# A decoder layer's cross attention: steps of two key chunks for one query block, one PSUM bank for the values, three for the other matmuls

## The reference

```
x = x + self_attention(layernorm(x))          # rotary, causal, one head of 128
x = x + cross_attention(layernorm(x), ctx)    # 16 heads of 64, keys and values from ctx, then Wo and a bias
x = x + ffn(layernorm(x))                     # rounded to 127 levels, ternary weights, bias
```

## Time and profile before

| | us |
|---|---|
| median of 3 runs | 1188.72 (1188.53 to 1189.51) |
| the profiled execution | 1185.61 |
| its span, first to last instruction | 1183.6 |
| busy: PE, DVE, ACT, POOL | 1141.1, 931.6, 692.8, 231.7 |
| granted TensorE clock, mean | 0.986 |

### The profile page before, as it was taken

One profiled execution on the slowest core, in us unless ns is written; L12 is line 12 of the kernel. 1 busy time (PEld: TensorE's weight loads), 2 busy tenths in 40 slices (PEclk: granted clock), 3 DMA queues, 4 the chain that ended last, 5 costly groups with the idle time before them and its releaser, 6 DMA issues.

```text
span 1183.6 us, 20273 instructions
## 1 busy us (share of the span) xinstructions
PE 1141.1 (96%) x6561; PEld 1043.3 (88%) x6561; DVE 931.6 (79%) x1625; ACT 692.8 (59%) x969; POOL 231.7 (20%) x228
## 2 busy tenths in 40 slices
PE   6799999999999999999999999999999999999996
PEld 5578999998998888998999989999899998999996
DVE  3698788887888788787878878887788888878544
ACT  1155656656565665656656565665656566575762
POOL 3120130312213022130302213030221313012010
PEclk9799999999999999999999999999999999999997
DMA  6101010010101001010010101001010100100000
GB/s 149 40 1 41 2 40 4 1 43 3 41 3 41 4 2 40 3 41 4 10 34 1 40 5 40 4 4 40 2 41 3 41 3 2 42 2 1 3 1 4
DMA packets 12727, 24.40 MB, mean 21 GB/s; under 512 B 4934, under 2 KB 8654, under 8 KB 12494
## 3 DMA queue, kind: packets, MB, share of 16 engines
q1 hardware_dynamic: 12622, 23.00, 7.3%
HBM read 21.88 MB, written 0.82 MB: 19 GB/s over the span
## 4 chain that ended last, share of the span: by engine, by line
PE 90%; DVE 5%; issue 3%; ACT 1%; DMA 1%; POOL 0%; DVEq 0%; SPq 0%; POOLq 0%; ACTq 0%
PE banks L1075 34%; PE banks L1107 30%; PE banks L929 11%; PE banks L967 4%; PE banks L920 4%; PE banks L949 1%; PE banks L1091 1%; DVE pr_lo L877 1%; DVE maxes L660 1%; PE banks L1010 1%; PE banks L1000 0%; DMA q_hi<-negmaxT 0%; PE banks L1038 0%; PE banks L979 0%; DVE cN_hi L772 0%
## 5 line engine op out<-in xcount | busy, mean ns | idle before, releaser
L609 ACT ACTIVATE pr_hi<-banks 128x800 fp32r<-128x800 f32 x384 | 322.4, 840 | 398.7 <-PE banks L1075 398.7
L660 DVE TENSOR_REDUCE maxes<-banks 128x1 f32<-128x482 f32 x585 | 373.7, 653 | 61.4 <-PE banks L929 58.6
L877 DVE TENSOR_TENSOR pr_lo<-banks,pr_hi 128x800 fp32r<-128x800 f32 x352 | 346.8, 985 | 67.3 <-ACT banks L611 66.6
L611 ACT ACTIVATE banks<-banks 128x800 f32<-128x800 f32 x384 | 319.9, 833 | 0.0
L929 PE MATMUL banks<-cT_hi,q_hi 96*128 96x482 f32 x585 | 224.2, 383 | 4.8 <-DVE maxes L660 2.4
L1075 PE MATMUL banks<-q_hi,cT_hi 97*128 97x400 f32 x768 | 217.0, 364 | 8.9 <-DMA q_hi<-negmaxT 6.8
L1075 PE MATMUL banks<-q_hi,cT_lo 96*128 96x400 f32 x768 | 208.0, 352 | 0.0
L1075 PE MATMUL banks<-q_lo,cT_hi 96*128 96x400 f32 x768 | 204.2, 347 | 0.0
L1107 PE MATMUL banks<-pr_hi,cN_hi 128*97 128x400 f32 x704 | 186.7, 346 | 0.0
L1107 PE MATMUL banks<-pr_lo,cN_hi 128*97 128x400 f32 x704 | 185.3, 344 | 0.0
L1107 PE MATMUL banks<-pr_hi,cN_lo 128*96 128x400 f32 x704 | 185.2, 344 | 0.0
(11 more groups left out here) (117 smaller groups left out, 870.6 us busy)
## 6 DMA issues: line engine op xcount, KB each, us to landing
cT_raw<-in_ctxT SPq DMA_DIRECT2D x16, 568.5 KB
cN_raw<-in_ctx SPq DMA_DIRECT2D x16, 528.0 KB
out<-result SPq DMA_DIRECT2D x16, 50.0 KB
X<-in_x SPq DMA_DIRECT2D x1, 700.0 KB
cN_raw<-in_ctx_last SPq DMA_DIRECT2D x16, 40.5 KB
wqT<-in_wqT SPq DMA_DIRECT2D x1, 512.0 KB, 5.4
wo<-in_wo SPq DMA_DIRECT2D x1, 512.0 KB, 12.9
wkT<-in_wkT SPq DMA_DIRECT2D x1, 384.0 KB, 7.0
```

Source lines behind the costliest of these rows:

```text
L609: nc.scalar.activation(pr_hi[:, s % RING, :].rearrange("p (a q) -> p a q", a=2), pair, ACT.Exp, scale=float(DH) ** -0.5).then_inc(hi_done, 1)
L611: nc.scalar.activation(pair, pair, ACT.Exp, scale=float(DH) ** -0.5).then_inc(exp_done, 1)
L660: nc.vector.tensor_reduce(maxes[:, t, p:p + 1], here[:, 0:PW], AX.X, ALU.max).then_inc(misc_free, 1)
L877: nc.vector.tensor_tensor(low[rows, s % RING, :].rearrange("p (a q) -> p a q", a=2), banks[rows, slot:slot + 2, 0:BLK], pr_hi[rows, s % RI ...
```

## The change

A step becomes two key chunks for one query block of 400 columns. There are still 24 steps a batch, now 4 blocks of BSTEPS = 6. The values of a block need one bank (OUT, 4), so bank 5 (SIDE) joins the ring of the fills, which has FILLS = 3 banks: a fill waits for the one three before it. The first step of a block holds the short chunk and a full one: its values are 4 matmuls and its subtract is two instructions of 400 columns. ACT evicts 97x400 after steps 1, 7, 13 and 19. o_sb is doubled (one for even, one for odd batches), and the eviction no longer waits for "y". In the last batch sums and yh come in four quarters, three of them in the body (steps 10, 11, 16, 17, 21, 22) and one in TAIL. The start-up before batch 0 keeps its two banks.

```diff
-    NP = Q // PAIR
-    STEPS = NP * NCH
+    NB = Q // BLK
+    BSTEPS = NCH // 2
+    STEPS = NB * BSTEPS
+    FILLS = 3
...
-        o_sb = sb("o_sb", [DC + 1, Q])
+        o_sb = two("o_sb", [DC + 1, Q])
...
-        ST, OUT, MISC = 0, 4, 6
+        ST, OUT, MISC, SIDE = 0, 4, 6, 5
...
+        RINGED = [SIDE, MISC + 1, MISC]
...
-        for s, what, j in ((16, "sums", 0), (17, "yh", 0), (19, "yh", 1)):
+        for s, what, j in ((10, "sums", 0), (11, "yh", 0), (16, "sums", 1), (17, "yh", 1), (21, "sums", 2),
+                           (22, "yh", 2)):
...
-        TAIL = [("sums", 1), ("yh", 2), ("yh", 3), ("T3", 0), ("F", 0)]
+        TAIL = [("sums", 3), ("yh", 3), ("T3", 0), ("F", 0)]
...
+        def ring_bank(use):
+            return RINGED[(use - NSTART) % FILLS]
...
-        def chunk(s):
-            return (s + FULL) % NCH
+        def chunk(s, i):
+            return (2 * (s % BSTEPS) + i + FULL) % NCH
...
-            def evacuate(n, pair, y_use=None):
-                act.wait_ge(pv_done, n * STEPS + (pair + 1) * NCH)
-                if y_use is not None:
-                    act.wait_ge(misc_ready, y_use + 1)
-                nc.scalar.activation(o_sb[:, pair * PAIR:(pair + 1) * PAIR].rearrange("p (a q) -> p a q", a=2),
-                                     banks[0:DC + 1, OUT:OUT + 2, 0:BLK], ACT.Copy).then_inc(o_evac, 1)
+            def evacuate(n, par, blk):
+                act.wait_ge(pv_done, n * STEPS + (blk + 1) * BSTEPS)
+                nc.scalar.activation(o_sb[par][:, blk * BLK:(blk + 1) * BLK], banks[0:DC + 1, OUT, 0:BLK],
+                                     ACT.Copy).then_inc(o_evac, 1)
...
+                    if s % BSTEPS == 0:
+                        rows = slice(LOW_AT, LOW_AT + REST)
+                        nc.vector.tensor_tensor(pr_hi[rows, s % RING, 0:BLK], banks[rows, slot, 0:BLK],
+                                                pr_hi[rows, s % RING, 0:BLK].bitcast(F32), ALU.subtract)
+                        nc.vector.tensor_tensor(pr_lo[:, s % RING, BLK:PAIR], banks[:, slot + 1, 0:BLK],
+                                                pr_hi[:, s % RING, BLK:PAIR].bitcast(F32),
+                                                ALU.subtract).then_inc(lo_done, 1)
                     else:
...
-                if behind in INPUT.get(what, ()):
-                    pe.wait_ge(misc_free, use)
+                near = [away for away, before in enumerate(behind) if before in INPUT.get(what, ())]
+                if near:
+                    pe.wait_ge(misc_free, use - near[0])
                 else:
-                    at_least(pe, misc_free, use - 1)
+                    at_least(pe, misc_free, use - ring + 1)
...
             def values(b, par, s, i):
+                blk, first = s // BSTEPS, s % BSTEPS == 0
...
+                if i == 0:
+                    if first:
+                        at_least(pe, o_evac, b * NB + blk)
+                    pe.wait_ge(hi_done, b * STEPS + s + 1)
+                if i == 2:
+                    pe.wait_ge(lo_done, b * STEPS + s + 1)
+                for a in range(2):
+                    c = chunk(s, a)
...
+                    if c == FULL:
+                        if i < 2:
+                            continue
+                        e = pr_hi
+                    mm = nc.tensor.matmul(banks[0:m, OUT, 0:BLK], k, e[:, r, cols], start=(first and a == 1 and i == 0),
+                                          stop=(s % BSTEPS == BSTEPS - 1 and a == 1 and i == 2))
```

More of the change, by code:

```diff
@@ L966, in fill @@
                     for h in range(H):
-                        mm = nc.tensor.matmul(here[0:S, 0:D], o_sb[0:DC, h * S:(h + 1) * S], G[:, h, :],
+                        mm = nc.tensor.matmul(here[0:S, 0:D], o_sb[par][0:DC, h * S:(h + 1) * S], G[:, h, :],
                                               start=(h == 0), stop=(h == H - 1))
                 elif what == "sums":
[L971 to L974, removed]
+                    pe.wait_ge(o_evac, n * NB + j + 1)
+                    for i in range(4):
+                        q0 = (4 * j + i) * S
+                        mm = nc.tensor.matmul(here[0:S, i:i + 1], o_sb[par][DC:DC + 1, q0:q0 + S],
                                               cT_hi[par][DC:DC + 1, 0:1].bitcast(F32), start=True, stop=True)
@@ L978, in fill @@
                         h = 4 * j + i
-                        mm = nc.tensor.matmul(here[0:S, i * D:(i + 1) * D], o_sb[0:DC, h * S:(h + 1) * S], G[:, h, :],
+                        mm = nc.tensor.matmul(here[0:S, i * D:(i + 1) * D], o_sb[par][0:DC, h * S:(h + 1) * S], G[:, h, :],
                                               start=True, stop=True)
@@ L991, in start @@
                 k = START.index((what, n))
-                behind = START[k - 1][0] if k else None
+                behind = [START[k - 1][0]] if k else []
                 if what == "q":
-                    fill(0, 0, what, n, k, MISC + k % 2, behind)
+                    fill(0, 0, what, n, k, MISC + k % 2, behind, 2)
                 else:
-                    fill(n, n, what, 0, k, MISC + k % 2, behind)
+                    fill(n, n, what, 0, k, MISC + k % 2, behind, 2)
             def m_bank(j):
@@ L1080, in values @@
             def values(b, par, s, i):
[L1082 to L1095, removed]
+                blk, first = s // BSTEPS, s % BSTEPS == 0
+                r = s % RING
+                if s == 0 and i == 0:
                     pe.wait_ge(cNhi_done, b + 1)
                     pe.wait_ge(cNlo_done, b + 1)
+                    pe.wait_ge(last_done, b + 1)
                 if i == 0:
+                    if first:
+                        at_least(pe, o_evac, b * NB + blk)
                     pe.wait_ge(hi_done, b * STEPS + s + 1)
@@ L1101, in values @@
                     pe.wait_ge(lo_done, b * STEPS + s + 1)
[L1102 to L1105 removed]
                 for a in range(2):
[L1107 to L1108 removed]
+                    c = chunk(s, a)
+                    cols = slice(a * BLK, (a + 1) * BLK)
+                    terms = [(cN_hi[par][:, c, 0:DC + 1], pr_hi, DC + 1), (cN_lo[par][:, c % FULL, :], pr_hi, DC),
+                             (cN_hi[par][:, c, 0:DC + 1], pr_lo, DC + 1)]
+                    k, e, m = terms[i]
+                    if c == FULL:
[4 more added lines that the diff above has]
+                                          stop=(s % BSTEPS == BSTEPS - 1 and a == 1 and i == 2))
                 if i == 2:
@@ L1127, in body @@
                             fill(b + away, par if away % 2 == 0 else 1 - par, what, j, use, bank, behind)
-                            behind = what
+                            behind = [what] + behind[:FILLS - 2]
             batches(pe, body)
@@ L1134, in _ @@
             for k, (what, j) in enumerate(TAIL):
-                fill(B - 1, 1, what, j, base(B) + k, MISC + (base(B) + k) % 2, TAIL[k - 1][0] if k else None)
+                fill(B - 1, 1, what, j, base(B) + k, ring_bank(base(B) + k), [TAIL[k - 1][0]] if k else [])
 def kernel(x, ctx_768, L0_attn_wq, L0_attn_wk, L0_attn_wv, L0_xattn_Wq, L0_xattn_Wk, L0_xattn_Wv,
```

71 lines of the change are left out of this document (32 added, 39 removed).

## The result

The changed kernel takes 1173.56 us (1172.84 to 1173.88, 4 runs) against 1188.62 for the kernel before; ratio 0.9876, interval 0.9861 to 0.9892. Run again on another chip (e12) it took 1172.78 against 1184.44, 0.9895 (0.9877 to 0.9914). It is faster, and by more than forecast: 1180.3 was forecast, and the result lies under the range's lower end, 1174.5. The profiled execution took 1173.88, its span 1170.9, 12.7 us less than before. One execution each of e4 (1249 us), of e10 (1864 us) and of the kernel before beside e1 to e4 (1261 us) ran at a much lower granted clock, and the ratios leave them out.

A forecast was written before the change was run, and what follows sets the result against it. TensorE's matmul stream was taken to bound the kernel. Terms 4.0 + 0.8 + 1.4 + 0.8 + 0.5 - 0.3 + 0.4 + 0.8 took 8.4 off span 1183.6; adding 2.0 and 3.1 gave 1180.3 us, range 1174.5 to 1190.

The forecast's parts named there:

- The offset: Runs' median over the profiled execution: 3.1 us in the kernel before, added to 1177.2 to give 1180.3.
- The 13 distances: Time from the loop's first negated-maxima issue to the fourteenth, 906.00 us before; forecast to lose 4.0, 1.4 and 0.8.
- The three L960 holes: Attention output's matmuls waiting for a max reduction behind long last_chunk rows; the third bank saves 4.0 us.
- the turn: Loop turns: the ring gives nothing by itself, the longer first value step nets 0.24 at each of 6, 1.4 us.
- The hole of 2.20 us: TensorE's hole at the first turn into the loop, at 107.65; the ring saves 0.8 us, bounds 0.4 to 2.0.
- VectorE, which then sets the pace: Batch 0, with 18 maxima more: ring depth helps only what is uneven, 0.5 us, bounds 0 to 2.
- From the fourteenth issue to the end: Last batch and tail: 0.4 us from value loads' eviction waits, net 0.8 from output work moved into the batch.
- Rival D: All waits for maxes, q_lo and the loop's lag go: 13.9 us less, 1174.8 us; chance 0.13.
- Same-bank accumulation: Value matmuls into the bank of the one before: taken as 0, bounds 0 to +10 ns each, 0 to +22 us.
- four evictions: ScalarE's evictions, 4 a batch of about 0.50 against 2 of 0.833: +0.34 us a batch, costing nothing.
- VectorE's extra time: Two subtracts in a block's first step: +0.50 us a batch, +8.0 in all, mostly hidden behind TensorE's stream.
- rival B: VectorE's two subtract halves land where TensorE waits, in every block: 8.0 us uncovered, 1188.3 us; chance 0.15.

The follow-up runs named there:

- e12: The changed kernel as it is, run again on another chip; 1172.78 us, ratio 0.9895.
- e4: The changed kernel with two quarters of the last batch's sums and yh at steps 16 to 19, the other two behind the last step; 1172.01 us, ratio 0.9869.
- e10: e5 with one maximum moved from step 8 to step 2 and one from step 20 to step 14; 1189.69 us, ratio 1.0042.
- e1: The changed kernel with its three fill banks, but a fill again waits for the one two before it; 1194.78 us, ratio 1.0061.
- e2: The kernel before with last_chunk issued after step 8 in place of step 10; 1181.80 us, ratio 0.9951.
- e5: The changed kernel with fills waiting two back and last_chunk at step 8 in place of 10; 1188.64 us, ratio 1.0025.
- e9: e5 with the subtract of a block's first step as one instruction of 128x800; 1182.48 us, ratio 0.9977.
- e3: The changed kernel with last_chunk after step 8 in place of step 10; 1172.54 us, ratio 0.9874.
- e6: e2 with o_sb doubled and the eviction's wait for y taken away; 1180.72 us, ratio 0.9953.

## Why the prediction was wrong

The direction was right and so were the parts that move; the sizes of several terms and one offset were not. The miss is 6.7 us: 4.3 of the span, 3.4 of the offset, less 1.0 because the profiled execution has 3.0 us around its span and not 2.0.

**The offset, 3.4 us.** That "the median of the runs, 1188.72, lies 3.1 above the profiled one" was added to the forecast as if it belonged to the measurement. The changed kernel's median lies 0.3 under its profiled run (1173.56, 1173.88), which was forecast at 1177.2. The 3.1 belongs to the kernel before, whose runs differ by their collisions: with the collisions away (e2) the spread shrinks from 8.7 to 2.9 us. That the profiled execution had fewer than the others is likely, and not shown.

**The sum, 4.3 us short.** By the three stretches of the trace:
- The 13 distances: 6.2 forecast (4.0 + 1.4 + 0.8), 7.82 found. The three L960 holes were right, 4.2. The step that failed is the turn: "So the ring gives nothing here by itself", net 0.24 at each of 6 turns, 1.4. There are five, and their distances lose 0.5 to 0.7 each, 3.0 in all. At the turn behind 268 the wait for q_lo went, 0.55 us, and the wait for pr_lo behind it grew by 0.08 only, from 0.34 to 0.42. The forecast had VectorE 0.13 us slower before this wait; it is 0.20 faster. Its pr_lo begins 4.46 us after it resumes in the kernel before (273.80 to 278.26), 4.26 in the changed one (271.67 to 275.93). 0.11 of it lies in its two maxima, which fits that the late L929 had held up the second; the rest was not tracked down. The seven other distances without a turn in them, from the second on, lose some 0.14 each beside the L960 holes, 1.0 in all (0.8 forecast), and in the first a long row of last_chunk gives 0.4 back.
- The start and batch 0: 0.5 + 0.8 - 0.3 forecast, 2.38 found. The hole of 2.20 us is 1.51 long now, and its stretch is 0.70 shorter (0.8 forecast). "VectorE, which then sets the pace" in batch 0 was wrong: 1.7 us came from there, 0.5 less 0.3 was forecast. It is the ring that gives it: batch 0's own negmaxT issue comes at 96.1 to 96.8 us in all kernels with fills two back, e1, e5, e9 and e10 with the new step among them, and at 94.3 to 94.7 in all with three back.
- From the fourteenth issue to the end: 1.2 forecast, 2.50 found, and the surplus is the chance of one profile. Against e2 the changed step has just the forecast size (147.34 us in e2, 146.14 in e3). The profile of the kernel before has 1.3 us more there than e2: a last_chunk of 1.86 us at 1071.10, which costs 0.5 us, and TensorE's clock, which fell in the tail and cost 0.8 (last section). The tail itself, from the last eviction's start to the end of the last multiply-add, went from 7.5 to 4.1 us (6.7 in e2) where 2.8 less was forecast.

```profile
277.16 0.19 PEld L929 LDWEIGHTS banks<-cT_hi,q_hi 96*128 96x128 f32 x1 [0.55 <-DVE q_lo L655]
```

```profile
276.96 0.30 PEld L1086 LDWEIGHTS banks<-q_hi,cT_hi 97*128 97x128 f32 x2 [0.42 <-DVE pr_lo L887]
```

Rival D, that all waits for maxes, q_lo and the loop's lag go, had 7.7 us for the 13 distances, where 7.82 were found, and 2 us for batch 0, where 1.7 were; its 1174.8 us is the nearest of the recorded times, though it holds the same wrong offset.

**The steps that held.** Same-bank accumulation is free (1.10 us for six). The doubled o_sb gives nothing (e6), and four evictions cost nothing: TensorE's loads of values wait for them 0.4 us in 2 places, 2.0 in 8 before. VectorE's extra time is hidden, but only by the third bank: it is 0.18 us a block and not 0.13, and with fills waiting two back it costs 4.1 us in the 13 distances (e5 against e9). So rival B had a real mechanism, which the third bank kept from showing, at about 0.3 us a batch where the rival took 0.5. What the forecast missed is that the ring's worth is not the holes seen before, some 8 us, but those and the ones that the new step would have opened. e5 less e3 is 16.1 us by the medians (on two chips); by the profiles it is 11.3 in the 13 distances, 4.8 up to the first of them, of which about 1.5 is the clock, and 0.8 at the end.

The rule of the Trainium skill (SBUF — State Buffer, section "Who interferes with whom") agrees with the runs: with last_chunk away from GpSimd's work every row is 0.31 us (e2), beside it up to 2.78 (e12). For the product with o_sb the order fits it too. The prediction saw last_chunk begin 0.03 us ahead of cN_lo and took this for an exception; but the product had begun 3.59 us earlier and was still running, so last_chunk was already the later one. Why cN_lo then still comes before it in the long rows, the rule does not say and no run here settles.

Open: which part of TensorE's new order makes up the other 3.3 of e5's 7.4 us. e10 moved the wait and did not remove it.

## What to carry to other kernels

Holes in the trace of before are not the measure of what more slack is worth: when the same change makes the consumer later, price the change once with the slack and once without. When a kernel's runs spread, look for an instruction whose length differs from batch to batch (0.31 to 2.41 us here), and for what another engine is running when it starts, before adding the spread to a forecast. A loop's jump back is a fixed cost (1.5 to 1.7 us here) that shows as alternating distances between equal batches, and writing the batches out takes it away.

## What the runs showed of the hardware

Behind the hole at the first turn TensorE's clock can fall. In e2's profile the hole is 2.20 us long; behind it the windows are granted 0.59, then 0.99, and 400-column matmuls start 0.333 us apart (1.2 GHz) until 112.4.

```profile
105.00:108.00 3.00, 1.45 (x8) 1.00 (x6) 2.00 (x4) 1.57 (x2) 1.17 (x3) 1.00 0.00 0
108.00:112.00 4.00, 3.71 (x12) 3.39 (x13) 3.02 (x5) 1.01 (x2) 0.00 (x0) 0.59 0.00 0
112.00:116.00 4.00, 4.00 (x23) 3.74 (x22) 3.41 (x6) 2.96 (x4) 0.00 (x0) 0.99 0.00 0
```

Of the six profiles with a hole of 2.10 or 2.20 us there, four show the fall (e2, e5, e6, e10; granted 0.59 to 0.73 from 108 to 112) and two do not (before, e1). The four have last_chunk at step 8 and the two at step 10, so the kernel and not chance may decide it. The kernels whose fills wait three back (holes of 1.50 or 1.51 us) and e9 (1.79) have no fall. It takes about 1.5 us: from batch 0's negmaxT issue to the first in the loop there are 34.37 in e2, against 32.84 before.

The clock can fall in the tail too. There TensorE stands 1.02 us for the last eviction behind a full stream, then works 16 one-column matmuls of sums in 1.47 us and 16 of yh (L979). In the profile of the kernel before, the clock falls to 0.50 (1.2 GHz) as yh begins; in e2's it stays up through nearly all of yh. First before, then e2, each with a window inside yh:

```profile
1171.15 3.51 PE L979 MATMUL banks<-G,o_sb 96*100 96x128 f32 x16
...
1172.00:1173.00 1.00, 1.00 (x7) 1.00 (x6) 0.01 (x1) 0.00 (x0) 0.00 (x0) 0.50 0.00 0
```

```profile
1168.55 2.15 PE L979 MATMUL banks<-G,o_sb 96*100 96x128 f32 x16
...
1169.00:1170.00 1.00, 1.00 (x12) 1.00 (x11) 0.29 (x1) 0.00 (x0) 0.00 (x0) 1.00 0.00 0
```

From the eviction's start to the last multiply-add this makes 7.5 us against 6.7. In e6 the clock falls already during the sums and it is 8.1. The changed kernel stands 0.69 us there, and its 8 matmuls of yh take 1.12 us.

These two falls fit the two groups of runs of e2 and e6. e2's profile has the first fall and a span of 1180.2, e6's has both and 1181.0; with 1.5, and 1.5 + 1.4, taken off they come to 1178.7 and 1178.1 (an estimate), which is the lower group, 1177.9 to 1178.6, within 0.1 us. That the falls are the cause is likely and not shown: the other runs have no trace, and their mean granted clock, 0.987 to 0.990 in the lower group and 0.985 to 0.989 in the upper, overlaps. e10's profile has the first fall and yet lies among the faster of its runs.
